# Prologue in another order: input transposes first, low part of the input in two steps, first half's norm ahead of the second half's weights

## The reference

```
x = x + layernorm(attn(layernorm(x)))
x = x + layernorm(ffn(layernorm(x)))
```

```
q_mid  = rmsnorm(x @ q_a_w.T) ; q = q_mid @ q_b_w.T
kv_a   = x @ kv_a_w.T         ; kv = rmsnorm(kv_a[:, :64]) @ kv_b_w.T ; k_pe = kv_a[:, 64:]
main   = softmax(q k.T / sqrt(192)) v @ o_w.T
pattern= softmax(pq pk.T / 4) pv @ sp_o_w.T
out    = gates[0] * main + gates[1] * pattern,  gates = softmax(x @ gate_w.T + gate_b)
```

## Time and profile before

| | |
|---|---|
| median of 3 runs | 868.13 us (868.11, 868.13, 871.94) |
| the profiled execution's own time | 870.45 us |
| its span, first to last instruction | 868.7 us |
| PE busy in the span | 802.5 us (92%) |
| DVE / ACT / POOL busy | 590.9 / 398.4 / 430.6 us |
| mean granted TensorE clock | 0.972 |
| first instruction of the attention | 53.95 us |

### The profile page before, as it was taken

The page is one execution under the profiler, slowest core; times in us unless marked ns, Lnnn a source line. Parts: engine busy times, 40 slices in busy tenths (PEclk is TensorE's granted clock), DMA queues, the critical chain, the costliest instruction groups (busy, mean ns, idle before and its releaser), DMA issues. The chain is left out here.

```text
span 868.7 us, 12785 instructions
## 1 busy us (share of the span) xinstructions
PE 802.5 (92%) x4964; PEld 463.8 (53%) x4964; DVE 590.9 (68%) x680; ACT 398.4 (46%) x499; POOL 430.6 (50%) x255
## 2 busy tenths in 40 slices
PE   5878988999999999999999999999999997999885
PEld 5663554455555554555555545545555553468754
DVE  3745765766677576856785776677666889874646
ACT  3332444555455545554555555555545553520321
POOL 1414209654856574468439552865485543530222
PEclk9979999999999999999999999999999999899978
DMA  9479462007201620351044105300621018101001
GB/s 246 175 203 286 76 169 30 10 14 147 62 1 36 112 62 2 72 114 49 13 98 114 34 13 132 71 19 14 116 62 50 25 51 312 40 14 61 0 1 49
DMA packets 92704, 68.52 MB, mean 79 GB/s; under 512 B 61858, under 2 KB 71396, under 8 KB 92388
## 3 DMA queue, kind: packets, MB, share of 16 engines
q1 hardware_dynamic: 92644, 67.71, 30.2%
HBM read 42.02 MB, written 17.04 MB: 68 GB/s over the span
## 5 line engine op out<-in xcount | busy, mean ns | idle before, releaser
L966 POOL TENSOR_TENSOR acc<-acc,em 128x1024 f32<-128x1024 f32 x96 | 237.2, 2470 | 96.5 <-ACT em L1024 96.4
L1117 DVE TENSOR_REDUCE m2p<-xb 128x2 f32<-128x1024 f32 x128 | 155.2, 1220 | 77.5 <-PE xb L1281 77.1
L1125 DVE TENSOR_REDUCE m<-xb 128x2 f32<-128x1024 f32 x128 | 155.7, 1219 | 63.1 <-PE xb L1281 63.0
L1015 ACT ACTIVATE ep<-xb 128x1024 f32<-128x1024 f32 x128 | 131.1, 1024 | 111.7 <-PE xb L1281 111.7
L1024 ACT ACTIVATE em<-xb 128x1024 f32<-128x1024 f32 x128 | 131.1, 1024 | 102.0 <-PE xb L1281 92.5
L1316 PE MATMUL pvm<-em,cpair 128*64 128x512 f32 x512 | 138.3, 618 | 7.4 <-ACT ctxr L1070 7.4
L929 POOL TENSOR_TENSOR rot<-rot,sin 128x512 f32<-128x512 f32 x32 | 40.9, 1278 | 116.2 <-DMA rot<-raw 116.2
L1281 PEld LDWEIGHTS xb<-pq,pk 49*128 49x128 f32 x256 | 23.9, 184 | 101.0 <-issue 81.3
L966 POOL TENSOR_TENSOR acc<-em 128x1024 f32<-128x1024 f32 x16 | 38.1, 2378 | 64.7 <-PE xb L1424 50.9
L1327 PE MATMUL pvp<-ep,vp 128*32 128x512 f32 x512 | 69.1, 612 | 0.0
L1281 PE MATMUL xb<-pq,pk 49*128 49x512 f32 x256 | 64.3, 499 | 0.0
(11 more groups left out here) (282 smaller groups left out, 1297.3 us busy)
## 6 DMA issues: line engine op xcount, KB each, us to landing
rot<-raw SPq DMA_DIRECT2D x128, 64.0 KB, 2.0
pk<-spqk_d SPq DMA_DIRECT2D x48, 128.0 KB, 4.3
sums<-rec_d SPq DMA_DIRECT2D x32, 128.0 KB, 2.9
ctx_d<-ctxr SPq DMA_DIRECT2D x14, 256.0 KB, 2.0
pq<-spqk_d SPq DMA_DIRECT2D x48, 64.0 KB, 2.3
wraw<-wst_d SPq DMA_DIRECT2D x7, 384.0 KB, 5.8
em<-in_o_w SPq DMA_DIRECT2D x1, 2048.0 KB, 7.8
vp<-vp_d SPq DMA_DIRECT2D x8, 256.0 KB, 4.8
```

The costliest lines, as they stand in the source:

```text
L966: pool.tensor_tensor(acc[:, :, :], before, em[:, j:j + 2, :], ALU.add).then_inc(added, 1)
L1015: act.activation(ep[:, j:j + 2, :], src[:, :, :], ACT.Exp, scale=PAT_SCALE).then_inc(ep_ready, 1)
L1117: dve.tensor_reduce(m2p[:, t, 2 * tp:2 * tp + 2, kt], src[:, :, :], AX, ALU.max).then_inc(x_dve, 1)
L1125: dve.tensor_reduce(m2[:, q, t, :, kt], src[:, :, :], AX, ALU.max).then_inc(x_dve, 1)
```

## The change

The list of jobs gets another order, and what hangs on jobs moves with it. Line numbers shift by a few.

- The input transposes follow right after `w1T`, with `spT(0)` and `spT(1)` between and behind them; all `kpT` come later, two after the fourth `proj1`, one before and one after the pattern jobs of the keys. `xT(0, 0)` and `xT(1, 0)` are still evacuated by ACT; `kpT(0, 1)` is the only `kpT` left to ACT.
- `cT(0)`, `qm0T(0)`, `qm1T(0)` come before `pe0T(1)`.
- The high part `xh` is made in two instructions, for feature half 0 after `proj1(3)` and half 1 after `proj1(7)`. The low part `xl` is made in two instructions of 128x1024, one after each of POOL's two root chains.
- `normalise(1)` moves behind DVE's evacuation of `lat0(0)`, and the gates move from the end of DVE's stream to a place behind it.

```diff
-    jobs = [("w1T", k) for k in range(NK)] + [("spT", 0), ("spT", 1)]
-    jobs += [("kpT", k, 0) for k in range(NK)] + [("xT", k, 0) for k in range(NK)]
-    jobs += [("kpT", k, 1) for k in range(NK)] + [("xT", k, 1) for k in range(NK)]
-    jobs += [("proj1", t) for t in range(NT)]
-    jobs += [("spqk", 1, 0), ("spqk", 1, 1), ("spqk", 0, 0), ("spT", 2)]
-    for q in range(2):
-        jobs += [("pe0T", q), ("pe1T", q), ("lat0", q), ("lat1", q)]
-    for q in range(2):
-        jobs += [("cT", q), ("qm0T", q), ("qm1T", q)]
+    jobs = [("w1T", k) for k in range(NK)] + [("xT", k, 0) for k in range(NK)] + [("spT", 0)]
+    jobs += [("xT", k, 1) for k in range(NK)] + [("spT", 1)]
+    jobs += [("proj1", t) for t in range(4)] + [("kpT", 0, 0), ("kpT", 0, 1)] + [("proj1", t) for t in range(4, NT)]
+    jobs += [("kpT", 1, 0), ("spqk", 1, 0), ("spqk", 1, 1), ("kpT", 1, 1), ("spqk", 0, 0), ("spT", 2)]
+    jobs += [("pe0T", 0), ("pe1T", 0), ("lat0", 0), ("lat1", 0), ("cT", 0), ("qm0T", 0), ("qm1T", 0)]
+    jobs += [("pe0T", 1), ("pe1T", 1), ("lat0", 1), ("lat1", 1), ("cT", 1), ("qm0T", 1), ("qm1T", 1)]
...
-            pool.wait_ge(xh_ready, 1)
-            evacuated(pool, index[("xT", 1, 1)])
-            pool.tensor_tensor(g["xl"][:, :, :], xT[:, :, :], g["xh"][:, :, :].bitcast(F32), ALU.subtract).then_inc(xl_ready, 1)
+                if q == 0:
+                    evacuated(pool, index[("xT", 1, 1)])
+                pool.wait_ge(xh_ready, q + 1)
+                pool.tensor_tensor(g["xl"][:, q, :], xT[:, q, :], g["xh"][:, q, :].bitcast(F32),
+                                   ALU.subtract).then_inc(xl_ready, 1)
...
+                if job in (("proj1", 3), ("proj1", 7)):
+                    k = job[1] // 4
+                    evacuated(act, index[("xT", k, 1)])
+                    act.activation(g["xh"][:, k, :], xT[:, k, :], ACT.Copy).then_inc(xh_ready, 1)
                 if job == ("spqk", 0, 0):
-                    act.activation(g["xh"][:, :, :], xT[:, :, :], ACT.Copy).then_inc(xh_ready, 1)
                     act.wait_ge(logits, 1)
...
                 if job == ("spqk", 0, 0):
-                    for q in range(2):
-                        normalise(q)
+                    normalise(0)
+                if job == ("lat0", 0):
+                    normalise(1)
+                    dve.wait_ge(gexp, 1)
+                    link(dve.tensor_reduce(gsum[:, :], gl[:, :, :], AX, ALU.add))
...
```

More of the change, by code:

```diff
@@ L53, in prologue @@
 def prologue(nc, a, d, g):
-    jobs = [("w1T", k) for k in range(NK)] + [("spT", 0), ("spT", 1)]
-    jobs += [("kpT", k, 0) for k in range(NK)] + [("xT", k, 0) for k in range(NK)]
-    jobs += [("kpT", k, 1) for k in range(NK)] + [("xT", k, 1) for k in range(NK)]
-    jobs += [("proj1", t) for t in range(NT)]
-    jobs += [("spqk", 1, 0), ("spqk", 1, 1), ("spqk", 0, 0), ("spT", 2)]
-    for q in range(2):
-        jobs += [("pe0T", q), ("pe1T", q), ("lat0", q), ("lat1", q)]
-    for q in range(2):
-        jobs += [("cT", q), ("qm0T", q), ("qm1T", q)]
+    jobs = [("w1T", k) for k in range(NK)] + [("xT", k, 0) for k in range(NK)] + [("spT", 0)]
[4 more added lines that the diff above has]
+    jobs += [("pe0T", 1), ("pe1T", 1), ("lat0", 1), ("lat1", 1), ("cT", 1), ("qm0T", 1), ("qm1T", 1)]
     index = {j: n for n, j in enumerate(jobs)}
     split = ("spqk", "cT", "qm0T", "qm1T")
-    act_jobs = [("w1T", 0), ("w1T", 1), ("spT", 0), ("spT", 1), ("kpT", 0, 0), ("kpT", 1, 0), ("xT", 0, 0),
-                ("xT", 1, 0), ("kpT", 1, 1), ("xT", 1, 1), ("spT", 2), ("pe1T", 0), ("lat1", 0), ("pe1T", 1), ("lat1", 1)]
+    act_jobs = [("w1T", 0), ("w1T", 1), ("xT", 0, 0), ("xT", 1, 0), ("spT", 0), ("xT", 1, 1), ("spT", 1), ("kpT", 0, 1),
+                ("spT", 2), ("pe1T", 0), ("lat1", 0), ("pe1T", 1), ("lat1", 1)]
     by_act = [j in act_jobs for j in jobs]
@@ L413, in _ @@
                 if job == ("spqk", 0, 0):
-                    for q in range(2):
-                        normalise(q)
+                    normalise(0)
[3 more added lines that the diff above has]
+                    link(dve.tensor_reduce(gsum[:, :], gl[:, :, :], AX, ALU.add))
+                    link(dve.reciprocal(gsum[:, :], gsum[:, :]))
+                    link(dve.tensor_tensor(gates[:, :, :], gl[:, :, :], gsum[:, :].unsqueeze(2).broadcast_to((P, NT, 2)),
+                                           ALU.mult))
                 if job == ("lat1", 0):
@@ L420, in _ @@
                                            wst[:, 0, 0:6, :].rearrange("p c j -> p (c j)").bitcast(F32), ALU.subtract))
[L421 to L425, removed]
 def pattern_weights(g):
```

## The result

The changed kernel takes **864.2 us** (median of 6 runs, 863.23 to 865.56) against 868.49 (6 runs, 867.32 to 871.94): ratio 0.9937, 95% interval [0.9919, 0.9955]. Run again beside later experiments it took 862.43 us (6 runs) against 867.88 (15 runs): 0.9940 [0.9918, 0.9962]. The ratios are the recorded ones and not the quotients of these medians, which are 0.9951 and 0.9937 and lie within the intervals. So it is faster by some 0.6%: 4.3 us by the first pair of medians, 5.4 by the second, 5.2 to 5.5 by the ratios. Its profiled execution took 863.23 us, with a span of 861.4.

What follows compares the result with a forecast made beforehand. The prologue is bound by PE, DVE's last wall copy, store and barrier. Attention moves from 53.95 to 41.86 + 6.91 = 48.77, 5.18 us earlier: 868.13 - 5.18 = 862.95, so 863.0 us, range 860.0 to 866.5.

Steps and rivals of the forecast that it cites:

- band of 0.9 us: Whole kernel: time within about 0.9 us of 863.0, chance 0.47.
- rival 1: DVE's statistics and rmsnorm still held by POOL's xl: 863.9, or 865.6 with late clock; 0.28 together with unfavourable dip.
- unfavourable dip: First attention slot: one more PE clock dip, costing about 1.6 us, gives 864.6; chance 0.28 together with rival 1.
- T0: Start of PE's first projection: forecast to move from 19.28 to 14.86 us.
- T0 to N: First projection to DVE's first rmsnorm: projections, moved transposes, pattern jobs; rmsnorm at 30.27, no clock loss.
- rival 4: Projections and pattern jobs: PE's clock stays at 1.2 GHz, up to 876.9 us; slower, chance 0.03.
- The hold: POOL's xl blocking DVE's rmsnorm, 4.27 us: forecast gone, second half of xl ending 0.19 us ahead of it.
- N to C: DVE's first rmsnorm to the end of its last wall copy: 11.59 us forecast, 14.19 before.
- The store: End of DVE's last wall copy to attention start: issue, landing and barrier stay 6.91 us.
- Behind the prologue: From attention start on: the same program, so the 5.18 us gained earlier carries through.
- rival 2: First attention slot: one clock dip more or less, 864.6 or 861.4; shared chances 0.28 unfavourable, 0.17 favourable.
- rival 3: Prologue: clock rise at 13.1 and store landing in 5.9 give 1.3 us more, 861.6; 0.17 with favourable dip.

Runs made afterwards that it cites:

- e1: Kernel before with only xh and xl made in two early steps, old job order kept; 864.23 us, ratio 0.9947.
- e7: Kernel before with one wait changed, so POOL makes xl later, in one piece, where DVE only empties PSUM; 863.09 us, ratio 0.9952.
- e4: Kernel before with new job order up to spT(2) and early split of xh and xl, later DVE and PE work as before; 862.74 us, ratio 0.9932.
- e2: Changed kernel with xh and xl in one piece each after the third pattern job; 867.18 us, ratio 0.9993.
- e3: Kernel before with only the jobs up to spT(2) in the new order, xh and xl in one piece; 866.05 us, ratio 0.9977.
- after_again: Changed kernel run once more, unedited; 862.43 us median, ratio 0.9940, profiled execution 864.80 us.
- e6: New front; normalise(0) and second weights earlier, normalise(1) and gates behind the last wall copy, xl in one piece behind normalise(1); 858.4 us, ratio 0.9891.
- after_third: Changed kernel, unedited, third profiled execution; 862.91 us, one run.
- after: The changed kernel against the kernel before, first profiled execution 863.23 us; median 864.2 us, ratio 0.9937.

## Why the prediction was right, point by point

The time forecast was 863.0 by a gain of 5.18 us; the ratios put the gain at 5.2 to 5.5, the medians at 4.3 and 5.4. The measured 864.2 lies just above the band of 0.9 us around the forecast, where the chances had put rival 1 and the unfavourable dip; in the profiled execution neither occurred, as the steps show, and the kernel before stood at 868.49 beside it and not at the 868.13 of the base. In its steps:

- *T0*: forecast 14.86, measured 14.13, 15.02 and 14.14. The moment was forecast within 0.8 us, but the gain of 4.42 counts from the 19.28 of one execution. In the other two executions of the kernel before T0 was 17.52 and 17.18, and in e1 and e7, whose edits act only behind T0, 18.90 and 19.79. Against the two the gain is some 2.9; between the mean of all five and that of all eight with the new front, 18.53 and 14.60, it is 3.9. **This is the term that was mis-sized, by 0.5 to 1.5 us**: I took the 1.66 us of waiting, and the late rise of PE's rate behind it, for a property of the kernel, although the three runs shown differed by 3.8 us.
- *T0 to N*: forecast 30.27 - 14.86 = 15.41, measured 15.32 three times. The clock took nothing there, and rival 4 didn't occur. The argument for it was no good guide, though: the rise was put at 5.3 us after PE's start at 9.55, and with no pause of PE it came 2.6 us after the first full-size transpose in e4, between 12.21 and 13.70 in the change, and only behind T0, over 5.1 us after it, in e2 and e3, where T0 to N is 15.60 and 15.48. That the loss was nothing is in part luck.
- *The hold*: the margin between POOL and the rmsnorm was forecast as 0.19 us and measured as 0.24 (0.23 in after_again, 30.34 less 30.11). The rule of the Trainium skill, "SBUF — State Buffer", section "Who interferes with whom", spoke against rival 1, and the trace bears it out on both sides. Beside the first half of `xl` the statistics, one SBUF input, take their usual 0.60; the next instruction, with two, takes 0.73 instead of 0.14:

```profile
22.72 0.60 DVE L404 BATCH_NORM_STATS2 lstats<-m 128x6 f32<-128x64 f32 x4
23.36 0.38 DVE L407 BATCH_NORM_AGGREGATE lmv<-lstats 128x2 f32<-128x6 f32 x4
23.65 0.73 DVE L410 TENSOR_TENSOR gl<-m,gate_b 128x16 f32<-128x16 f32 x1
```

- *N to C*: forecast 11.59, measured 11.56. The 4.27 of the hold is confirmed by e7. The forecast had 1.68 of cost in it for the second part of the new order (2.65 for gates and splits, less 0.97 for the wait for ACT), and e4 confirms that with 1.64.
- *The store*: forecast 6.91, measured 5.90. I allowed 0 to 0.5 and took 0; it was 1.0, since the landing of 5.9 in the earlier trace rows belongs to the smaller store, so it was no lower bound for the bigger one once that stands alone.
- *Behind the prologue*: 816.5 before and 816.3 after in the profiled pair. Nothing is taken back, rival 2's dips notwithstanding; over all executions this part lies between 813.9 and 817.0, and that spread I have not explained.

So the mechanism was right, and two terms had wrong sizes: the gain at T0 0.5 to 1.5 us too big, the store's 1.0 too small. That they nearly cancel is luck. Both halves of rival 3 in fact came, an early rise (0.7 us in two of three executions) and a quicker store: the attention started at 46.91, 47.80 and 46.91, 1.0 to 1.9 us before the forecast 48.77. The time was still not 861.6, because the gain was counted from 53.95, in an execution of 870.45 us, and taken off the median of 868.13. The prediction saw that this execution was 2.32 us above the median and did not ask where; the two further executions, of 867.95 and 868.62 us, start the attention 2.1 us earlier. Mean against mean, the attention moved from 51.85 (those two) or 52.55 (all three) to 47.2, by 4.6 or 5.3 us.

## What to carry to other kernels

Read why one of several equal instructions is many times as long as the others: here it named the other engine, and moving that engine's one long instruction by one wait (e7) gave most of what the whole reordering gave. Place a long POOL instruction beside DVE work that reads PSUM, as e6 does, and check that a piece of it doesn't merely meet the next rmsnorm. Before pricing a wait for a transfer or a rise of PE's pace, look at it in more than one execution; and where a store ends a block, what counts is when its last input is ready and whether another store is still under way.

## What was not expected of the hardware

A 1536 KB store landed in 5.3 to 5.4 us alone and in 5.9 to 7.1 us when issued 3.3 to 3.9 us behind one of 1152 KB. The same 1024 KB load of `kpe_nat` landed 6.7 to 9.0 us after its issue in the thirteen profiled executions, 6.7 and 9.0 in two of one and the same kernel (after_third, after). And the granted-clock column reads 1.00 from the start in stretches where, by the durations, PE ran at half pace: here, in the changed kernel, 1.00 from 8 to 10 us, while the eight transposes from 9.59 took 1.76 us to the next row's start, and eight at the quick pace take 0.92.

```profile
8.00:10.00 2.00, 2.00 (x10) 1.41 (x9) 1.71 (x9) 0.69 (x2) 1.38 (x3) 1.00 1.08 375
```
